# Q projection moved from a stage of its own into the attention stage's scratch tiles, interleaved with the first K/V pair

## The chip, the cores and the metric

One Trainium2 chip, all 8 cores, one launch. Each core runs the same program on its own data; the time is device microseconds of the slowest core. In the text PE is TensorE (matmuls, PEld its weight loads), DVE VectorE, ACT ScalarE, POOL GpSimd and SP SyncE. All loads are issued by SP on one hardware DMA queue; all stores by POOL on another.

## The reference, cut to what matters

A transformer layer with post-norm, in float32: batch 4, 2048 positions, 2048 features, 16 heads of 128.

```python
def attn(x, W_qkv, W_o):
    q, k, v = split(x @ W_qkv, 3)           # 16 heads of 128
    a = q @ k.T / sqrt(128) + alibi + causal
    return (softmax(a) @ v) @ W_o
x = layernorm(x + attn(x, W_qkv, W_o))
x = layernorm(x + ffn(x))                   # dense 2048x2048 + 16 low-rank experts, top 2
```

Core c holds batch c//2 and half of its query positions (eight tiles of 128, alternating so that the causal work is even): 1024 "own" positions. Each core projects Q for its 1024 positions, and K and V for all 2048.

## The kernel before, in words

A recording layer writes one list of operations for each engine (`Prog`); the kernel's order in the source is the order on each engine, and each engine runs its list strictly in that order. `Buf` (lines 69 to 115) holds for a buffer the semaphore counts that its next writer must wait for: `load` waits on SP for all recorded uses, then issues `split` DMAs, all at line 107; `store` issues on POOL at line 117.

- **Q stage** (lines 215 to 265). The core's whole input `xT_own` (8 MiB) is loaded into `xq` in 4 DMAs of 2 MiB. For each of 16 heads (`oc`) the 1 MiB of Q weights goes into one of two `wqb` buffers, by 4 DMAs of 256 KB, and is used for two banks of 512 positions, 16 contraction steps each (line 247). DVE scales a bank into `qout` (line 258), POOL stores it to `q_hbm`. Each float32 matmul appears as two records in the trace, so 512 matmuls are 1024 records.
- **Barrier** (line 266, `phase_barrier(q_done)`): every engine waits for all matmuls, all DVE and ACT work and all stores to `q_hbm`. The tiles of the next stage take the same memory.
- **K/V stage and attention** (from line 268). The generator `kv_gen(g)` (line 296) computes K and V for a pair of heads. Its first step only issues loads: `wk` 2 MiB, `wv` 2 MiB and two tiles of the input, `xb` 0 and 1, 2 MiB each. Then follow 32 steps: for each of 8 position tiles `tb`, two K steps (line 338) and two V steps (line 362), each 16 matmuls of 256 columns into bank 6 or 7, followed by a DVE copy. `xb` has two buffers: after the last step of tile `tb`, SP waits until PE has done it, then loads tile `tb+2` over it. `kv_gen(0)` runs alone (lines 517 to 519). Then `attention(gh, gen)` (line 424) runs eight times, with the steps of the next pair's generator woven between its own matmuls. It first loads `qh`, one head of Q from `q_hbm` (512 KB, after `q_done`), and lets the generator issue its loads; then per key tile it multiplies K with `qh` (line 455), adds the table `posb`, takes the exponential and multiplies with V (403) and with ones (412).
- The output projection, the layer norms, the router, the experts and the dense layer follow; the change does not touch them.

```python
def load(self, dst, src, split=1):
    ...
    self.begin_write()          # SP waits for every recorded use
    for i in range(split):
        mk = self.p.op("sync", ... e.dma_start(...), self.sem, 16)
```

Of the kernel before, what the change touches and what calls it, by code (L numbers as in the profile page):

```python
# [7 lines left out]
F32 = mybir.dt.float32  # L8
F16 = mybir.dt.float16
AF = mybir.ActivationFunctionType  # L10
ALU = mybir.AluOpType
# [3 lines left out]
H = 16  # L15
# [3 lines left out]
OWN = 1024  # L19
# [9 lines left out]
INV_SQRT_DH = 1.0 / float(np.sqrt(np.float64(DH)))  # L29
EPS = 1e-5  # L30
NEG_BIG = -1e30
FCN = 16
D3 = 3 * D
# [92 lines left out]
def build_program():  # L126
    nc = bass.Bass("TRN2", target_bir_lowering=False)

    xT = nc.dram_tensor("xT", [D, S], F32, kind="ExternalInput")
    xT_own = nc.dram_tensor("xT_own", [D, OWN], F32, kind="ExternalInput")  # L130
    x_own = nc.dram_tensor("x_own", [OWN, D], F32, kind="ExternalInput")
    wqkv = nc.dram_tensor("wqkv", [D, D3], F32, kind="ExternalInput")
# [14 lines left out]
    q_hbm = nc.dram_tensor("q_hbm", [D, OWN], F32)  # L147
# [5 lines left out]
    p = Prog()  # L153
    MM, DV, AC = "s_mm", "s_dv", "s_ac"

    def dap(t, offset, dims):
        return bass.AP(t, offset, dims)

    with ExitStack() as g:
# [55 lines left out]
        with ExitStack() as ph:  # L215
            def pb(name, shape, dt=F32):
                return ph.enter_context(nc.sbuf_tensor(name, shape, dt))

            xq = pb("xq", [128, FCN * 1024])
            xqb = B("sync")  # L220
            wqb = [pb(f"wqb{i}", [128, FCN * 128]) for i in range(2)]
            wqbuf = [B("sync"), B("sync")]
            qout = [pb(f"qout{i}", [128, 512]) for i in range(2)]
            qoutbuf = [B("vector"), B("vector")]

            xqmk = xqb.load(
                [dap(xq, fc0 * 1024, [[FCN * 1024, 128], [1024, 4], [1, 1024]])
                 for fc0 in range(0, FCN, 4)],
                [dap(xT_own, fc0 * 128 * OWN, [[OWN, 128], [128 * OWN, 4], [1, 1024]])
                 for fc0 in range(0, FCN, 4)], split=4)  # L230

            for oc in range(H):
                wb, wbuf = wqb[oc % 2], wqbuf[oc % 2]
                wmk = wbuf.load(
                    [dap(wb, fc0 * 128, [[FCN * 128, 128], [128, 4], [1, 128]])
                     for fc0 in range(0, FCN, 4)],
                    [dap(wqkv, fc0 * 128 * D3 + oc * 128,
                         [[D3, 128], [128 * D3, 4], [1, 128]])
                     for fc0 in range(0, FCN, 4)], split=4)
                for tb in range(2):  # L240
                    bi = (oc * 2 + tb) % 8
                    bb = bankbuf[bi]
                    bb.begin_write()
                    p.wait("tensor", wmk)
                    p.wait("tensor", xqmk)
                    for fc in range(FCN):
                        mmk = p.op("tensor", (lambda bi_, fc_, oc_, tb_: (lambda e: e.matmul(  # L247
                            banks[bi_][:, 0:512],
                            wqb[oc_ % 2][:, fc_ * 128:(fc_ + 1) * 128],
                            xq[:, fc_ * 1024 + tb_ * 512: fc_ * 1024 + tb_ * 512 + 512],  # L250
                            start=(fc_ == 0), stop=(fc_ == FCN - 1))))(bi, fc, oc, tb),
                            MM if fc == FCN - 1 else None)
                    wbuf.use(mmk)
                    bb.ready = mmk
                    qo, qob = qout[tb % 2], qoutbuf[tb % 2]
                    qob.begin_write()
                    p.wait("vector", mmk)
                    emk = p.op("vector", (lambda qo_, bi_: (lambda e: e.tensor_scalar(
                        qo_[:, :], banks[bi_][:, 0:512], INV_SQRT_DH, None,
                        ALU.mult)))(qo, bi), DV)  # L260
                    bb.use(emk)
                    qob.store(dap(q_hbm, oc * 128 * OWN + tb * 512,
                                  [[OWN, 128], [1, 512]]),
                              qo[:, :], deps=[emk])
            q_done = [qoutbuf[0].st_total(), qoutbuf[1].st_total()]
        phase_barrier(q_done)

        with ExitStack() as ph:
            def pb(name, shape, dt=F32):
# [8 lines left out]
            K2 = [pb(f"K2_{i}", [128, 2 * 2048]) for i in range(2)]  # L278
            V2 = [pb(f"V2_{i}", [128, 16 * 256]) for i in range(2)]
            k2buf = [B("vector"), B("vector")]  # L280
            v2buf = [B("vector"), B("vector")]
            qh = [pb(f"qh{i}", [128, 1024]) for i in range(2)]
            qhbuf = [B("sync"), B("sync")]
            posb = [pb(f"posb{i}", [128, 1024]) for i in range(2)]
            posbuf = [B("sync"), B("sync")]
            st_sb = [pb(f"st_sb{i}", [128, 1024]) for i in range(2)]
            stbuf = [B("vector"), B("vector")]
# [226 lines left out]
                                   deps=[last_y])  # L514

            gen0 = kv_gen(0)
            for _ in gen0:
                pass
            for gh in range(8):
                nxt = kv_gen(gh + 1) if gh < 7 else None  # L520
                attention(gh, nxt)
                if nxt is not None:
                    for _ in nxt:
                        pass
            y_done = [yfmsgbuf.st_total()]
        phase_barrier(y_done)
        with ExitStack() as cde:
# [58 lines left out]
            with ExitStack() as ph:  # L586
# [26 lines left out]
                for oc in range(FCN):  # L613
                    wbuf = wocb[oc % 2]
                    wmk = wbuf.load(
                        [dap(wocol[oc % 2], fc0 * 128,
                             [[FCN * 128, 128], [128, 4], [1, 128]])
                         for fc0 in range(0, FCN, 4)],
                        [dap(wo, fc0 * 128 * D + oc * 128,
                             [[D, 128], [128 * D, 4], [1, 128]])  # L620
                         for fc0 in range(0, FCN, 4)], split=4)
                    for tb in range(2):
                        bi = (oc * 2 + tb) % 2
                        bb = bankbuf[bi]
# [3 lines left out]
                        for fc in range(FCN):  # L628
                            mmk = p.op("tensor", (lambda bi_, fc_, oc_, tb_: (lambda e: e.matmul(  # L629
                                banks[bi_][:, 0:512],  # L630
                                wocol[oc_ % 2][:, fc_ * 128:(fc_ + 1) * 128],
                                yfm_all[:, fc_ * 1024 + tb_ * 512: fc_ * 1024 + tb_ * 512 + 512],
                                start=(fc_ == 0), stop=(fc_ == FCN - 1))))(bi, fc, oc, tb),
                                MM if fc == FCN - 1 else None)
# [20 lines left out]
                            start=(oc_ == 0), stop=(oc_ == FCN - 1))))(oc, tb),  # L655
# [11 lines left out]
                            start=(oc_ == 0), stop=(oc_ == FCN - 1))))(sq, oc, tb),  # L667
# [6 lines left out]
                for tt in range(NSLOT):  # L674
                    bi = tt % 2
                    bb = bankbuf[bi]
# [23 lines left out]
            with ExitStack() as ph:  # L700
# [35 lines left out]
                for tb in range(2):  # L736
                    bi = 6 + tb % 2
                    bb = bankbuf[bi]
# [13 lines left out]
                    if h_evacs:  # L752
# [14 lines left out]
                for tt in range(NSLOT):  # L767
                    bi = tt % 2
                    bb = bankbuf[bi]
# [42 lines left out]
                for tt in range(NSLOT):  # L812
                    bi = 2 + tt % 2
                    bb = bankbuf[bi]
# [3 lines left out]
                    for fc in range(FCN):  # L818
# [4 lines left out]
                            start=(fc_ == 0), stop=(fc_ == FCN - 1))))(bi, fc, tt),  # L823
# [9 lines left out]
                    wmk = None  # L833
# [6 lines left out]
                    for c in range(2):  # L840
# [19 lines left out]
            with ExitStack() as ph:  # L860
# [21 lines left out]
                for oc in range(FCN):  # L882
                    wbuf = wtcb[oc % 2]
# [212 lines left out]
```

How the kernel before makes its waits and increments, by code:

```python
            def run(e):  # L996
                for item in lst:
                    if item[0] == "wait":
                        e.wait_ge(sems[item[1]], item[2])
                    else:
                        _, fn, sem, by = item
                        ins = fn(e)
                        if sem is not None:
                            ins.then_inc(sems[sem], by)
```

## Time and profile before

| what | us |
|---|---|
| runs, median (lowest to highest of 3) | 5239.11 (4938.11 to 5711.35) |
| the profiled execution | 4931.57 |
| its span on the slowest core, core 0 | 4930.0 |
| spans of the 8 cores | 4892.6 to 4930.0 |
| PE busy, DVE busy, ACT busy on core 0 | 4225.8, 717.3, 411.6 |

The span runs from the first to the last instruction of one core; 1.6 us lie around it. Busy time is time in which an engine executes something; for PE it counts matmuls only. The granted clock of TensorE has two levels here, shown as 1.00 (2.4 GHz) and 0.50 (1.2 GHz); in a window it is a mean.

### The profile page before, as it was taken

How to read it: one execution, taken by the hardware profiler on the slowest of the kernel's cores; microseconds unless marked ns; L12 is line 12 of the kernel's file. 1: busy time of each engine (PE TensorE's matmuls, PEld its weight loads, DVE VectorE, ACT ScalarE, POOL GpSimd, SP SyncE). 2: the span in 40 equal slices, each digit the busy share in tenths (PEclk: the TensorE clock that was granted, in tenths of full speed). 3: DMA queues.
4: the chain of work that ended last, by engine and by line, in shares of the span. 5: the costliest groups of instructions: out<-in, count | busy, mean ns of one | idle time of the engine just before them, and what ended most of it. 6: DMA issues, size and time to landing. Idle time of an engine off the chain costs nothing.

```text
span 4930.0 us, 37169 instructions; the slowest of 8 cores (4892.6 to 4930.0 us)
## 1 busy us (share of the span) xinstructions
PE 4225.8 (86%) x14312; PEld 2728.1 (55%) x14312; DVE 717.3 (15%) x1152; ACT 411.6 (8%) x723; POOL 29.2 (1%) x56
## 2 busy tenths in 40 slices
PE   6998899879979989979989989977999556888882
PEld 3443787767767767767667767643344233333330
DVE  0000001111111111111111111130000332101115
ACT  0000001111111111111111111130000000000000
POOL 0000000000000000000000000000000000000000
PEclk9999999999999989999999999998999877889996
DMA  3211333232232232232232142123111001000001
GB/s 114 62 54 59 105 109 100 85 104 78 88 99 78 93 119 74 76 116 74 78 129 92 46 138 86 60 84 115 49 51 41 15 22 37 23 26 26 26 17 68
DMA packets 332846, 359.57 MB, mean 73 GB/s; under 512 B 16896, under 2 KB 293504, under 8 KB 332416
## 3 DMA queue, kind: packets, MB, share of 16 engines
q1 hardware_dynamic: 325696, 332.02, 21.5%
q0 software_dynamic: 6976, 25.17, 1.3%
q8 instruction: 116, 1.90, 0.2%
q14 instruction: 58, 0.48, 0.0%
HBM read 331.97 MB, written 25.17 MB: 72 GB/s over the span
## 4 chain that ended last, share of the span: by engine, by line
PE 84%; DVE 6%; SPq 4%; DMA 3%; issue 2%; ACT 0%; DVEq 0%; ACTq 0%; POOL 0%; POOLq 0%
PE bank L338 18%; PE bank L362 18%; PE bank L900 9%; PE bank L629 9%; PE bank L247 9%; PE bank L455 5%; PE bank L403 5%; PE bank L412 5%; SPq L107 4%; DMA xb<-xT 1%; PE bank L819 1%; DMA qh<-q_hbm 1%; PE bank L915 1%; PE bank L944 1%; PE bank L957 1%
## 5 line engine op out<-in xcount | busy, mean ns | idle before, releaser
L338 PE MATMUL bank<-xb,wk 128*128 128x256 f32 x4096 | 918.8, 384 | 156.4 <-DMA xb<-xT 156.4
L338 PEld LDWEIGHTS bank<-xb,wk 128*128 128x128 f32 x4096 | 790.8, 193 | 296.8 <-issue 187.2
L362 PE MATMUL bank<-wv,xb 128*128 128x256 f32 x4096 | 901.5, 379 | 0.0
L362 PEld LDWEIGHTS bank<-wv,xb 128*128 128x128 f32 x4096 | 775.0, 190 | 117.1 <-issue 3.3
L629 PE MATMUL bank<-yfm_all,wocol 128*128 128x512 f32 x1024 | 446.6, 594 | 41.1 <-DMA wocol<-wo 41.1
L900 PE MATMUL bank<-x1fm,wtcol 128*128 128x512 f32 x1024 | 470.1, 619 | 12.0 <-DMA wtcol<-wT 12.0
L247 PE MATMUL bank<-xq,wqb 128*128 128x512 f32 x1024 | 441.1, 594 | 38.5 <-DMA wqb<-wqkv 38.5
L455 PE MATMUL bank<-qh,K 128*128 128x512 f32 (+3 forms) x768 | 308.6, 512 | 81.3 <-DMA qh<-q_hbm 68.5
L900 PEld LDWEIGHTS bank<-x1fm,wtcol 128*128 128x128 f32 x1024 | 204.7, 200 | 277.7 <-issue 277.7
L629 PEld LDWEIGHTS bank<-yfm_all,wocol 128*128 128x128 f32 x1024 | 195.2, 191 | 286.8 <-issue 286.8
L247 PEld LDWEIGHTS bank<-xq,wqb 128*128 128x128 f32 x1024 | 195.1, 191 | 283.7 <-issue 283.7
L403 PE MATMUL bank<-pt_sb,V 128*128 128x512 f32 (+3 forms) x768 | 314.8, 492 | 32.9 <-ACT pt_sb L486 32.6
L486 ACT ACTIVATE pt_sb<-st_sb 128x1024 f32<-128x1024 f32 (+7 forms) x256 | 174.8, 683 | 1883.5 <-DVE st_sb L478 1883.5
L412 PE MATMUL bank<-pt_sb,ones_sb 128*128 128x512 f32 (+3 forms) x768 | 310.6, 486 | 0.0
L455 PEld LDWEIGHTS bank<-qh,K 128*128 128x128 f32 x768 | 149.3, 197 | 239.4 <-issue 228.6
L348 DVE COPY K<-bank 128x256 f32<-128x256 f32 x128 | 54.3, 424 | 1215.1 <-PE bank L338 1205.0
L478 DVE TENSOR_TENSOR st_sb<-st_sb,posb 128x1024 f32<-128x1024 f32 (+7 forms) x256 | 194.2, 759 | 149.0 <-ACT st_sb L465 101.6
L465 ACT COPY st_sb<-bank 128x512 f32<-128x512 f32 (+3 forms) x384 | 183.8, 479 | 333.2 <-PE bank L455 250.1
L372 DVE COPY V<-bank 128x256 f32<-128x256 f32 x128 | 54.3, 424 | 1037.9 <-PE bank L362 1018.9
L412 PEld LDWEIGHTS bank<-pt_sb,ones_sb 128*128 128x128 f32 x768 | 141.2, 190 | 112.4 <-issue 92.1
L403 PEld LDWEIGHTS bank<-pt_sb,V 128*128 128x128 f32 x768 | 138.9, 190 | 85.8 <-issue 63.7
L944 PE MATMUL bank<-x2fm,ones_sb 128*128 128x512 f32 x64 | 45.6, 802 | 85.3 <-DVE x2fm L935 85.3
(76 smaller groups left out, 932.6 us busy)
## 6 DMA issues: line engine op xcount, KB each, us to landing
xb<-xT SPq DMA_DIRECT2D x256, 512.0 KB, 6.5
wqb<-wqkv SPq DMA_DIRECT2D x64, 256.0 KB, 5.3
wk<-wqkv SPq DMA_DIRECT2D x32, 512.0 KB, 8.5
wv<-wqkv SPq DMA_DIRECT2D x32, 512.0 KB, 10.3
posb<-alibid SPq DMA_DIRECT2D x32, 512.0 KB, 8.7
wocol<-wo SPq DMA_DIRECT2D x64, 256.0 KB, 4.2
wtcol<-wT SPq DMA_DIRECT2D x64, 256.0 KB, 3.8
posb<-alibid SPq DMA_DIRECT2D x32, 448.0 KB, 3.3
```

Source lines behind the costliest of these rows:

```text
L107: mk = self.p.op("sync", (lambda d_, s_: (lambda e: e.dma_start(out=d_, in_=s_)))(dst[i] if split > 1 else dst, src[i] if split > 1 else s ...
L247: mmk = p.op("tensor", (lambda bi_, fc_, oc_, tb_: (lambda e: e.matmul(banks[bi_][:, 0:512], wqb[oc_ % 2][:, fc_ * 128:(fc_ + 1) * 128], x ...
L338: mmk = p.op("tensor", (lambda bi_, fc_, oc_, tb_, par_: (lambda e: e.matmul(banks[bi_][:, 0:256], wk_sb[par_][:, fc_ * 256 + oc_ * 128: f ...
L362: mmk = p.op("tensor", (lambda bi_, fc_, tt_, tb_, par_: (lambda e: e.matmul(banks[bi_][:, 0:256], xb[tb_ % 2][:, fc_ * 256 + tt_ * 128: f ...
L403: lambda e: e.matmul(banks[ybi_][:, co_: co_ + w_], V2[par_][:, kc_ * 256 + hd2_ * 128: kc_ * 256 + hd2_ * 128 + 128], pt_sb[kc_ % 2][:, r ...
L412: lambda e: e.matmul(banks[dbi_][:, co_: co_ + w_], ones_sb[:, :], pt_sb[kc_ % 2][:, ro_: ro_ + w_], start=st_, stop=sp_)))(dbi, kc, co, w ...
L455: lambda e: e.matmul(banks[bi_][:, 0:n_], K2[par_][:, hd2_ * 2048 + kc_ * 128: hd2_ * 2048 + kc_ * 128 + 128], qh[hd2_ % 2][:, s0_ * 128 + ...
L465: emk = p.op("scalar", (lambda bi_, kc_, ch_, n_: (lambda e: e.copy(st_sb[kc_ % 2][:, ch_ * 512: ch_ * 512 + n_], banks[bi_][:, 0:n_])))(b ...
L478: stmk = p.op("vector", (lambda kc_, w_: (lambda e: e.tensor_add(st_sb[kc_ % 2][:, 0:w_], st_sb[kc_ % 2][:, 0:w_], posb[kc_ % 2][:, 0:w_]) ...
L486: exmk = p.op("scalar", (lambda kc_, w_: (lambda e: e.activation(pt_sb[kc_ % 2][:, 0:w_], st_sb[kc_ % 2][:, 0:w_], AF.Exp)))(kc, w), AC)
L629: mmk = p.op("tensor", (lambda bi_, fc_, oc_, tb_: (lambda e: e.matmul(banks[bi_][:, 0:512], wocol[oc_ % 2][:, fc_ * 128:(fc_ + 1) * 128], ...
L900: mmk = p.op("tensor", (lambda bi_, fc_, oc_, tb_: (lambda e: e.matmul(banks[bi_][:, 0:512], wtcol[oc_ % 2][:, fc_ * 128:(fc_ + 1) * 128], ...
```

## The change

The Q stage, its tiles and the barrier behind it are removed. Q is now computed inside the attention stage, between the generator's first step and its end:

- The own positions are taken in two passes (`qp`) of 512, each as two halves (`qq`) of 256 that lie in `K2[1]` and `V2[1]`, the K and V buffers that pair 1 will use later. Each half is 2 MiB, in 4 DMAs of 512 KB.
- Q weights go through the two `qh` tiles, cut into four quarter buffers (`wq4`) of 256 KB, one for each four contraction steps (`fq`). Since there are two passes, all Q weights are loaded twice: 32 MiB, not 16.
- Per head, quarter and half there are 4 matmuls of 256 columns, into bank 0 or 1. After each quarter one step of `kv_gen(0)` is emitted. The generator has 32 such steps, so they are used up in the first 8 heads of the first pass; the other 24 head passes have nothing between their matmuls.
- After the four quarters DVE scales both banks into `st_sb`, and POOL stores them to `q_hbm`.
- The second pass reloads `K2[1]` and `V2[1]` when the first pass's last matmuls are done.

```diff
-            for oc in range(H):
-                wb, wbuf = wqb[oc % 2], wqbuf[oc % 2]
...
-                    for fc in range(FCN):
-                        mmk = p.op("tensor", (lambda bi_, fc_, oc_, tb_: (lambda e: e.matmul(
-                            banks[bi_][:, 0:512],
...
-        phase_barrier(q_done)
...
             gen0 = kv_gen(0)
+            next(gen0, None)
+            xq2 = [B("sync"), B("sync")]
+            xqt = [K2[1], V2[1]]
+            wq4 = [B("sync") for _ in range(4)]
...
+            for qp in range(2):
+                for qq in range(2):
+                    xq2[qq].load(
...
+                for oc in range(H):
+                    for fq in range(4):
+                        wb = wq4[fq]
+                        wt, woff = qh[fq // 2], (fq % 2) * 512
+                        wmk = wb.load(
...
+                        for qq in range(2):
+                            if fq == 0:
+                                bankbuf[qq].begin_write()
+                            p.wait("tensor", wmk)
+                            p.wait("tensor", xq2[qq].ready)
+                            for sub in range(4):
+                                fc = 4 * fq + sub
...
+                                        banks[qq_][:, 0:256],
...
+                            qqlast[qq] = mmk
...
+                        wb.use(mmk)
+                        next(gen0, None)
+                    for qq in range(2):
...
+                        p.wait("vector", qqlast[qq])
...
+                        bankbuf[qq].use(emk)
...
+                for qq in range(2):
+                    xq2[qq].use(qqlast[qq])
             for _ in gen0:
                 pass
```

**SP, from the start.** Before, in the order of issue: the input for Q, the Q weights of all heads, then K/V weights and input tiles (`xq` is the own input, `wqb` the Q weights, `xb` the input tiles of K/V).

```order
L107 DMA xq<-xT_own 128x4x1024 x4
L107 DMA wqb<-wqkv 128x4x128 x8
L107 DMA wqb<-wqkv 128x4x128 [waits s_mm]
L107 DMA wqb<-wqkv 128x4x128 x3
L107 DMA wqb<-wqkv 128x4x128 [waits s_mm]
L107 DMA wqb<-wqkv 128x4x128 x3
```

Now (`K_1` and `V_1` hold the own input, `qh` the Q weights; the wait on `s_mm` is one for matmuls):

```order
L107 DMA wk<-wqkv 128x4x256 x4
L107 DMA wv<-wqkv 128x4x256 x4
L107 DMA xb<-xT 128x4x256 x8
L107 DMA K_1<-xT_own 128x4x256 x4
L107 DMA V_1<-xT_own 128x4x256 x4
L107 DMA qh<-wqkv 128x4x128 x4
L107 DMA xb<-xT 128x4x256 [waits s_mm]
L107 DMA xb<-xT 128x4x256 x3
L107 DMA qh<-wqkv 128x4x128 x4
L107 DMA xb<-xT 128x4x256 [waits s_mm]
L107 DMA xb<-xT 128x4x256 x3
```

The first Q weights moved behind 12 MiB of other loads, and each head's Q weights stand behind an input tile's reload.

**PE, at the boundary of the first two heads of the first pass.** Before, PE goes from bank to bank of the Q stage with double-buffered weights:

```order
L247 MATMUL bank2<-xq,wqb1 128x512 x15
L247 MATMUL bank3<-xq,wqb1 128x512 x16
L247 MATMUL bank4<-xq,wqb0 128x512 [waits b6l]
L247 MATMUL bank4<-xq,wqb0 128x512 x15
L247 MATMUL bank5<-xq,wqb0 128x512 x16
```

Now (line 496 of the changed kernel is the Q matmul, 309 the V matmul and 285 the K matmul of the generator; `b11l` is the load of the first quarter buffer, `s_dv` DVE's work):

```order
L496 MATMUL bank0<-K2_1,qh1 128x256 [waits b14l]
L496 MATMUL bank0<-K2_1,qh1 128x256 x3
L496 MATMUL bank1<-V2_1,qh1 128x256 x4
L309 MATMUL bank7<-wv0,xb0 128x256 [waits s_dv]
L309 MATMUL bank7<-wv0,xb0 128x256 x15
L496 MATMUL bank0<-K2_1,qh0 128x256 [waits s_dv,b11l]
L496 MATMUL bank0<-K2_1,qh0 128x256 x3
L496 MATMUL bank1<-V2_1,qh0 128x256 [waits s_dv]
L496 MATMUL bank1<-V2_1,qh0 128x256 x3
L285 MATMUL bank6<-xb1,wk0 128x256 [waits b8l]
```

The Q matmuls of the next head stand right behind the tile's last V step, and ahead of the next K step.

**SP, at the end of the Q work.** Before, the loads of pair 1 follow the last input tile of `kv_gen(0)`:

```order
L107 DMA xb<-xT 128x4x256 [waits s_mm]
L107 DMA xb<-xT 128x4x256 x3
L107 DMA qh<-q_hbm 128x1024
L107 DMA wk<-wqkv 128x4x256 x4
L107 DMA wv<-wqkv 128x4x256 x4
```

Now (`b15s` and `b16s` are the stores of Q):

```order
L107 DMA K_1<-xT_own 128x4x256 [waits s_mm]
L107 DMA K_1<-xT_own 128x4x256 x3
L107 DMA V_1<-xT_own 128x4x256 [waits s_mm]
L107 DMA V_1<-xT_own 128x4x256 x3
L107 DMA qh<-wqkv 128x4x128 x4
L107 DMA qh<-wqkv 128x4x128 [waits s_mm] x60
L107 DMA qh<-q_hbm 128x1024 [waits b15s,b16s,s_mm]
L107 DMA wk<-wqkv 128x4x256 x4
L107 DMA wv<-wqkv 128x4x256 x4
L107 DMA xb<-xT 128x4x256 x8
```

The loads of pair 1, which were issued while `kv_gen(0)` still ran, now stand behind all Q weights and behind the last store of Q.

## Rows read from the trace of the kernel before

**Rows 1.** The page: busy time by engine, and the chain that ended last.

```profile
...
PE 4225.8 (86%) x14312; PEld 2728.1 (55%) x14312; DVE 717.3 (15%) x1152; ACT 411.6 (8%) x723; POOL 29.2 (1%) x56
...
PE 84%; DVE 6%; SPq 4%; DMA 3%; issue 2%; ACT 0%; DVEq 0%; ACTq 0%; POOL 0%; POOLq 0%
...
```

**Rows 2.** Waits of PE over the span (total us, times, longest us).

```profile
...
PE bank L338 <- DMA xb<-xT: 156.4, 7, 31.9
...
PE bank L247 <- DMA wqb<-wqkv: 38.5, 1, 38.5
...
```

**Rows 3.** Timeline from the start (start us, length us, operation).

```profile
...
3.19 7.38 SPq L107 DMA_DIRECT2D xq<-xT_own  x4
...
38.45 21.83 PE L247 MATMUL bank<-xq,wqb 128*128 128x512 f32 x47 [38.45 <-DMA wqb<-wqkv]
...
```

**Rows 4.** Timeline, end of the Q stage and start of K/V.

```profile
...
469.54 10.03 PE L247 MATMUL bank<-xq,wqb 128*128 128x512 f32 x23
...
479.75 0.69 DVE L258 TENSOR_SCALAR qout<-bank 128x512 f32<-128x512 f32 x1 [13.04 <-PE bank L247]
480.98 0.54 POOL L117 DMA_DIRECT2D q_hbm<-qout  x1 [13.20 <-DVE qout L258]
483.44 2.82 SPq L107 DMA_DIRECT2D wk<-wqkv  x4
...
511.48 16.17 PE L338 MATMUL bank<-xb,wk 128*128 128x256 f32 x64 [31.90 <-DMA xb<-xT]
...
527.48 13.98 PE L362 MATMUL bank<-wv,xb 128*128 128x256 f32 x64
...
541.29 13.98 PE L338 MATMUL bank<-xb,wk 128*128 128x256 f32 x64
541.63 0.42 DVE L372 COPY V<-bank 128x256 f32<-128x256 f32 x1 [6.48 <-PE bank L362]
...
```

**Rows 5.** Windows (us, busy us and records by engine, PEclk, DMA share, GB/s).

```profile
...
54.00:480.00 426.00, 425.58 (x992) 188.10 (x990) 21.67 (x32) 0.00 (x0) 16.92 (x31) 1.00 0.18 54
480.00:512.00 32.00, 0.53 (x1) 0.50 (x2) 0.45 (x1) 0.00 (x0) 0.54 (x1) 0.53 0.77 236
1991.00:1999.00 8.00, 0.01 (x1) 0.00 (x0) 6.93 (x4) 0.00 (x0) 0.22 (x1) 0.67 1.02 366
2001.00:2006.00 5.00, 5.00 (x16) 3.44 (x15) 0.00 (x0) 1.17 (x2) 0.00 (x0) 0.70 0.09 34
...
```

**Rows 6.** DMA of the stretch 500 to 520 us, in 40 slices.

```profile
...
GB/s 313 311 303 248 272 254 256 225 301 358 285 272 332 317 264 270 348 311 145 139 233 274 309 303 358 385 381 385 320 178 129 31 20 0 0 0 0 0 0 0
...
```

**Rows 7.** Timeline of SP, 540 to 552 us: one tile is reloaded.

```profile
...
541.54 2.60 SPq L107 DMA_DIRECT2D xb<-xT  x4
```

**Rows 8.** DMA of the stretch 540 to 552 us, in 40 slices.

```profile
...
GB/s 0 0 0 0 0 0 0 0 0 0 0 27 38 38 113 140 181 160 167 222 314 359 369 375 389 379 386 382 379 358 348 348 355 338 358 300 157 10 0 0
...
```

**Rows 9.** Timeline, 512 KB queued behind a tile, first of four.

```profile
...
919.77 3.19 SPq L107 DMA_DIRECT2D xb<-xT  x4
...
933.48 3.75 PE L455 MATMUL bank<-qh,K 128*128 128x512 f32 x4 [11.52 <-DMA qh<-q_hbm]
...
```

**Rows 10.** Timeline, the same, last of four.

```profile
...
1988.82 2.03 SPq L107 DMA_DIRECT2D xb<-xT  x4
...
1999.17 3.75 PE L455 MATMUL bank<-qh,K 128*128 128x512 f32 x4 [8.15 <-DMA qh<-q_hbm]
...
2010.25 1.88 PE L455 MATMUL bank<-qh,K 128*128 128x512 f32 x4
...
```

**Rows 11.** Timeline, start of attention for pair 1.

```profile
...
1065.82 0.43 SPq L107 DMA_DIRECT2D qh<-q_hbm  x1
...
1066.30 2.18 SPq L107 DMA_DIRECT2D wk<-wqkv  x4
...
1070.89 1.96 PE L455 MATMUL bank<-qh,K 128*128 128x512 f32 x4 [0.70 <-DMA qh<-q_hbm]
...
1095.49 16.00 PE L338 MATMUL bank<-xb,wk 128*128 128x256 f32 x64 [22.65 <-DMA xb<-xT]
...
```

**Rows 12.** The tile of the Q weights over the Q stage.

```profile
...
DMA to landing us min/median/max: 3.0/5.3/23.9
```

More of the change, by code:

```diff
@@ L213, in build_program @@
         zeromk = (DV, p.count[DV])
[L215 to L230, printed above, removed]
-            for oc in range(H):
-                wb, wbuf = wqb[oc % 2], wqbuf[oc % 2]
[L234 to L245, printed above, removed]
-                    for fc in range(FCN):
-                        mmk = p.op("tensor", (lambda bi_, fc_, oc_, tb_: (lambda e: e.matmul(
-                            banks[bi_][:, 0:512],
[L249 to L265, printed above, removed]
@@ L516, in build_program @@
             gen0 = kv_gen(0)
+            next(gen0, None)
+            xq2 = [B("sync"), B("sync")]
+            xqt = [K2[1], V2[1]]
+            wq4 = [B("sync") for _ in range(4)]
+            qo2 = [B("vector"), B("vector")]
+            qqlast = [None, None]
+            for qp in range(2):
+                for qq in range(2):
+                    xq2[qq].load(
+                        [dap(xqt[qq], fc0 * 256,
+                             [[4096, 128], [256, 4], [1, 256]])
+                         for fc0 in range(0, FCN, 4)],
+                        [dap(xT_own, fc0 * 128 * OWN + qp * 512 + qq * 256,
+                             [[OWN, 128], [128 * OWN, 4], [1, 256]])
+                         for fc0 in range(0, FCN, 4)], split=4)
+                for oc in range(H):
[3 more added lines that the diff above has]
+                        wmk = wb.load(
+                            dap(wt, woff, [[1024, 128], [128, 4], [1, 128]]),
+                            dap(wqkv, (4 * fq) * 128 * D3 + oc * 128,
+                                [[D3, 128], [128 * D3, 4], [1, 128]]))
+                        mmk = None
+                        for qq in range(2):
[5 more added lines that the diff above has]
+                                fc = 4 * fq + sub
+                                mmk = p.op("tensor", (lambda qq_, wt_, wo_, s_, fc_: (
+                                    lambda e: e.matmul(
+                                        banks[qq_][:, 0:256],
+                                        wt_[:, wo_ + s_ * 128: wo_ + s_ * 128 + 128],
+                                        xqt[qq_][:, fc_ * 256:(fc_ + 1) * 256],
+                                        start=(fc_ == 0), stop=(fc_ == FCN - 1))))(
+                                            qq, wt, woff, sub, fc),
+                                    MM if sub == 3 else None)
+                            qqlast[qq] = mmk
+                            if fq == 3:
+                                bankbuf[qq].ready = mmk
+                        wb.use(mmk)
+                        next(gen0, None)
+                    for qq in range(2):
+                        qob = qo2[qq]
+                        qob.begin_write()
+                        p.wait("vector", qqlast[qq])
+                        emk = p.op("vector", (lambda qq_: (lambda e: e.tensor_scalar(
+                            st_sb[qq_][:, 0:256], banks[qq_][:, 0:256],
+                            INV_SQRT_DH, None, ALU.mult)))(qq), DV)
+                        bankbuf[qq].use(emk)
+                        qob.store(dap(q_hbm, oc * 128 * OWN + qp * 512 + qq * 256,
+                                      [[OWN, 128], [1, 256]]),
+                                  st_sb[qq][:, 0:256], deps=[emk])
+                for qq in range(2):
+                    xq2[qq].use(qqlast[qq])
@@ L517, in build_program @@
             for _ in gen0:
                 pass
+            qlast = qqlast[1]
+            k2buf[1].use(qqlast[0])
+            v2buf[1].use(qqlast[1])
+            qhbuf[0].use(qlast)
+            qhbuf[1].use(qlast)
+            stbuf[0].use(qo2[0].st_total())
+            stbuf[1].use(qo2[1].st_total())
+            q_done = [qo2[0].st_total(), qo2[1].st_total()]
             for gh in range(8):
```

## The prediction

> **What bounds the kernel now.** I read the chain of waits first: it is PE for 84% of the span, and PE is busy for 4225.8 of 4930.0 us [rows 1]. So a change pays only where PE stands idle, and costs wherever it makes PE idle. The waits of PE say where: it waits 38.5 us at the very start for the first Q weights, and 156.4 us in 7 pieces for input tiles, the longest 31.9 us [rows 2]. The timeline puts that longest piece where the Q stage ends and K/V begins [rows 4]. In between PE has no gap: 425.58 of 426.00 us are busy, at the full granted clock, with the DMA engines used at 0.18 [rows 5]. The Q stage is thus hidden perfectly once it runs, and what can be won is the gap in front of it and the one behind it.
>
> **The removed barrier: -34.1 us.** The last Q matmuls end at 469.54 + 10.03 = 479.6 and the first K matmul starts at 511.48 [rows 4], 31.9 us. The clock is granted at 0.53 in that stretch [rows 5], and the first 64 records afterwards take 527.48 - 511.48 = 16.00 us, where the next 64 take 541.29 - 527.48 = 13.81: 2.2 us more. All of it goes, because K/V's loads now start with the kernel.
>
> **Narrower matmuls: +2.7.** Before, 992 records of 512 columns take 425.58 us, 0.429 each [rows 5], so 1024 take 439.3. Now there are 2048 of 256 columns, at 13.81 / 64 = 0.2158 [rows 4]: 442.0. Loading weights for half as many columns costs nothing, since the K and V steps already do just that. K and V themselves keep their 32 steps of 6.9 us.
>
> **The start: +14.5.** Before, 9 MiB are issued from 3.19 and PE starts at 38.45 [rows 3], 3.9 us per MiB. In the new order the first Q weights stand behind 12 MiB. The 8 MiB of 1 KB rows that begin at 483.44 [rows 4] have all come by 516.0, where the DMA falls silent [rows 6]: 4.1 us per MiB. For 12.25 MiB at 4.0 to 4.1 that is 49 to 50 us, so PE starts near 53 instead of 38.45. Bounds: 51 and 60 (the first 6 MiB at 483.44 needed 28.0 us until PE could start, 4.7 each).
>
> The Trainium skill, page "DMA: Bandwidth & Descriptors", section "Bandwidth", holds that two cores streaming from one HBM get about 358 GB/s each. By that figure, an estimate, 12.25 MiB would be in after 36 us and the start would cost nearly nothing: 5032 in all. The measured stretch moved 8 MiB in 32.6 us, some 257 GB/s, and the trace disagrees with the page here, so the sum doesn't use it.
>
> **Six stalls behind tile reloads: +76.8.** This is the largest term. During the first 8 heads the order is: last V step of tile tb, then, on SP, the wait for it, four DMAs of the next `xb` (2 MiB), and only then the first quarter of the next head's Q weights. On PE the very next instruction needs that quarter. A double-buffered tile that used to have 27.6 us to arrive now stands in front of something wanted at once. How long is that? When a tile is freed, at 541.29, SP issues the reload at 541.54 [rows 7], and the transfer ends in the slice at 551.1 [rows 8], 9.6 us later; 256 KB more at the 350 GB/s of those slices is 0.75, so the quarter is there 0.25 + 9.6 + 0.75 = 10.6 us after PE ran out. There is a direct model too: four times in the attention stage the 512 KB of `qh` are queued right behind a tile. From the tile's issue to PE's start it takes 933.48 - 919.77 = 13.7 us the first time [rows 9] and 1999.17 - 1988.82 = 10.35 the last [rows 10], the other two lie between. A load of `qh` that had nothing ahead of it was used after 5.1 us (1065.82 to 1070.89) [rows 11]. I take 10.6, bounds 9.5 and 13.7.
>
> Such an idle time also lowers the clock. In the 8 us ahead of 1999.17 the granted clock averages 0.67, between the two levels 1.2 and 2.4 GHz, and it is 0.70 in 2001 to 2006, with PE busy all through [rows 5]. The 4 + 32 records from 1999.17 to 2010.25 take 11.1 us [rows 10], against 4 x 0.429 + 32 x 0.2158 = 8.6 at full clock: 2.5. Together with 2.2 above and 16.00 - 13.98 = 2.0 after 22.65 us [rows 11], I take 2.2 for each; bounds 0 and 2.8. Tiles 2 to 7 are reloaded so, before heads 1 to 6: 6 x (10.6 + 2.2) = 76.8. The later quarters of a head come less than a microsecond apart and have 10.4 us of work each before them.
>
> **Two waits for DVE: +2.8.** DVE takes the V copy first and the scaling of bank 0 after it, and PE's next group needs bank 0. The copy starts 0.34 us after PE goes on (541.63 against 541.29) and takes 0.42 [rows 4]; scaling 256 columns takes about the same, with a tenth for each hand-over 1.4 us in all. At heads 1 to 6 it lies under the DMA stall; before heads 7 and 8 it is bare. Later, 4 matmuls (1.7 us) of the other half cover it.
>
> **The 24 head passes with Q alone: 0.** Each needs 1 MiB in 13.8 us. A quarter is reloaded when its 8 matmuls end and is wanted 3 x 3.45 = 10.4 us later; 256 KB land in 5.3 us, at best 3.0 [rows 12]. The 16 MiB read twice hide there. The 23.9 us of the longest landing are from the crowded start.
>
> **The turn between the passes: +19.2.** Both input halves, 4 MiB, are reloaded, SP issuing the first when the first half's matmuls end, 1.7 us before PE runs out. The next Q quarter stands behind both. Between 9.6 us for 2 MiB and 28.0 for 6 MiB, 4.25 MiB take 18.5 to 20; less 1.5 is 17 to 18.5. I take 17, bounds 13 and 20, and 2.2 for the clock. Nothing is left of K/V to cover it.
>
> **The start of attention: +32.9.** Before, the loads for pair 1 were issued under `kv_gen(0)`. Now SP first waits for the last store of Q: 3.9 us from PE's end, by the same chain at 479.6, DVE at 479.75, POOL at 480.98, SP at 483.44 [rows 4], less 0.3 for the shorter scaling. Then `qh`, and 0.5 later `wk`, `wv` and the first tile, 6 MiB. Pair 1's own attention shows just this: `wk` issued at 1066.30, first K matmul at 1095.49, 29.2 us [rows 11]. So K starts 3.6 + 0.5 + 29.2 = 33.3 us after PE ran out, of which 1.7 are the scores in between; a wait of 0.9 us that stood here goes; the clock adds 2.2. This nearly equals the barrier's 34.1: that gap is moved, not removed.
>
> **The sum.** 14.5 - 34.1 + 2.7 + 76.8 + 2.8 + 19.2 + 32.9 = 114.8. On the profiled execution's 4931.57 us that is 5046, a ratio of 1.023. That execution is near the lowest of the three runs, 4938.11; their median of 5239.11 contains two that lie 6 and 16% higher, and nothing in a 4930 us span explains those, so I forecast the undisturbed time.
>
> **The rivals.**
> *The small load passes the big one.* The DMA engines might finish a quarter while the tile ahead is still written. The Trainium skill, page "DMA: Bandwidth & Descriptors", section "Queues, rings and completion order", warns that completion is not first-in, first-out for an issuing engine. Price: the quarter is issued 0.25 + 2.6 us after PE's end and lands 3.0 to 5.3 later, so a stall is 5.9 to 8.2 instead of 10.6: 5018 to 5032, 5025 in the middle. Against it: `qh` needed 10.35 to 13.7 behind a tile [rows 9, 10] and 5.1 alone [rows 11].
> *Not slower.* The stalls don't arise, because the reload moves under the preceding V step: then only 14.5 - 34.1 + 2.7 + 2.8 + 19.2 + 32.9 = 38 us remain, 4970, 0.8% above and within what can be told. Even with the turn and the start of attention hidden as well it would be 4917, so faster by over 2% gets a chance only for a cover that I don't see. For it: the DMA engines are idle for 80% of this stage. Against: SP's reload waits for the tile's last matmul, and the program puts nothing between that and the quarter. Where the stall falls below 8 us, this decides the verdict.
> *The quarters are too small.* If a 256 KB load takes 13.4 us instead of 5.3, each of 24 head passes waits 3 us: 72 us more, 5118. The median landing [rows 12] speaks against it, the first case in rows 9, 13.7 us with a tile in front, shows it isn't absurd.
>
> **How the numbers follow.** About 2% is what a measurement of this kernel can tell from no change, 98.6 us here, close to my sum. Forecast 0.72, of which 0.10 fall under the 2%; the passing load 0.12, of which 0.10 under; not slower 0.08, of which 0.02 faster; quarters too small 0.08. Slower 0.72, same 0.26, faster 0.02. The bounds together: stalls 9.5 to 13.7 give -7 to +19, the clock -13 to +4, the start -2 to +7, the turn -4 to +3, attention -4 to +3. Not all at once: 5015 to 5080 for the forecast alone; to reach most of the other cases 4995 to 5100.
>
> **What would show each step right or wrong.** In the profile after, PE should first start near 53 us; six waits of Q matmuls for `qh`'s weights should be 10 to 11 us each, 55 us apart; one of about 17 us should stand between the passes, near 575; there should be no wait in the solo head passes; and the wait for `xb` at the start of attention should be over 20 us, as for the other pairs. Q's matmuls should sum to 442 us, plus what the low clock adds. A first start near 40, or waits behind tiles under 8 us, would make the prediction wrong, and so would gaps of a few microseconds in every solo head pass.

## The result and the profile after

The kernel became slower. Timed against the kernel before, the ratio is 1.018 (95% interval 1.010 to 1.026); timed again with the experiments it was 1.017 (1.009 to 1.025). Both intervals lie above 1, and both hold 1.02, so whether the loss is more than 2% stays open. The medians are 5211.3 us (8 runs, 5039.4 to 5784.2) against 5116.1 (10 runs, 4926.5 to 5711.4). Both medians, but not the ratio, include executions in which the cores of one die (0 to 3 or 4 to 7) were granted a lower TensorE clock for much of the time, as cores 0 to 3 were in the profiled execution of the kernel after. I therefore read cores 4 to 7 and compare each with the same core before: 5002.2, 5026.5, 5002.2 and 5037.6 us against 4914.7, 4927.4, 4901.3 and 4913.6. That is +87.5, +99.1, +100.9 and +124.0, +103 us in the mean.

The groups of PE on core 5 of the kernel after (busy us, mean ns of one | idle us before, and its releaser), which answer to [rows 2, 5]:

```profile
...
L285 PE MATMUL bank<-xb,wk 128*128 128x256 f32 x4096 | 921.8, 385 | 144.7 <-DMA xb<-xT 144.7
L309 PE MATMUL bank<-wv,xb 128*128 128x256 f32 x4096 | 902.8, 379 | 0.0
...
L496 PE MATMUL bank<-K,qh 128*128 128x256 f32 x1024 | 256.9, 396 | 142.7 <-DMA qh<-wqkv 139.9 <-DVE st_sb L512 2.8
L496 PE MATMUL bank<-V,qh 128*128 128x256 f32 x1024 | 245.6, 383 | 0.0
...
```

Q is the two rows of L496. Its matmuls are busy for 256.9 + 245.6 = 502.5 us, where the overlap of neighbours is counted to both rows (a group of 8 records lasts 1.89 us in the timeline, but the next starts after 1.73, and 256 groups at 1.73 make 442). The K and V rows, 921.8 and 902.8 us, had 921.7 and 901.4 on this core before. The new thing is the idle time: 139.9 us on loads of Q weights into `qh` and 144.7 on `xb`, where the same core of the kernel before had 37.9 and 162.0.

Each wait of Q for its weights is visible in the timeline of PE on the same core (start, length, operation, idle before it):

```profile
...
53.62 3.66 PE L496 MATMUL bank<-K,qh 128*128 128x256 f32 x8 [53.62 <-DMA qh<-wqkv]
...
111.31 3.75 PE L496 MATMUL bank<-K,qh 128*128 128x256 f32 x8 [14.32 <-DMA qh<-wqkv]
...
167.10 3.75 PE L496 MATMUL bank<-K,qh 128*128 128x256 f32 x8 [12.25 <-DMA qh<-wqkv]
...
222.53 3.75 PE L496 MATMUL bank<-K,qh 128*128 128x256 f32 x8 [10.78 <-DMA qh<-wqkv]
...
387.05 3.75 PE L496 MATMUL bank<-K,qh 128*128 128x256 f32 x8 [10.62 <-DMA qh<-wqkv]
...
432.34 1.97 PE L496 MATMUL bank<-K,qh 128*128 128x256 f32 x8 [1.39 <-DVE st_sb L512]
...
602.33 3.75 PE L496 MATMUL bank<-K,qh 128*128 128x256 f32 x8 [16.17 <-DMA qh<-wqkv]
...
```

And further on, at the start of attention:

```profile
...
823.80 1.89 PE L496 MATMUL bank<-V,qh 128*128 128x256 f32 x8
834.65 3.75 PE L402 MATMUL bank<-qh,K 128*128 128x512 f32 x4 [8.96 <-DMA qh<-q_hbm]
857.20 16.72 PE L285 MATMUL bank<-xb,wk 128*128 128x256 f32 x64 [18.79 <-DMA xb<-xT]
...
```

This is the order of the forecast. PE starts at 53.6 us. Six times, 54 to 58 us apart, the next head's first Q matmul waits for its quarter; two of the six, at 278.28 with 11.51 us and at 332.61 with 10.65, are left out. Then come two bare waits for DVE of 1.39 us (the first is shown), the wait between the passes, and at the start of attention one for `qh` and one for `xb`. The 3.75 us of the 8 records behind each DMA wait against 1.97 us behind the wait for DVE show the low clock after a gap: the 5 to 6 us behind the gaps that end at 111.31, 167.10 and 387.05 were granted 0.65, 0.54 and 0.61, and the 3.5 us from 432.34 on 1.00. On cores 4 to 7 the six waits sum to 66.8 to 72.0 us.

SP's row in one such gap shows the cause itself, the same core from 150 us on:

```profile
...
154.94 3.11 SPq L107 DMA_DIRECT2D xb<-xT  x4
158.09 6.62 SPq L107 DMA_DIRECT2D qh<-wqkv  x4
```

The tile is issued at 154.94, as soon as PE ran out (167.10 - 12.25 = 154.85), the quarters only from 158.09, and PE goes on 12.2 us after the tile's issue.

Finally the stages (us, busy us and records by engine, PEclk, DMA share, GB/s): the six gaps, the rest of the first pass, the second pass, attention.

```profile
...
54.00:432.00 378.00, 306.83 (x1344) 265.43 (x1343) 17.30 (x41) 0.00 (x0) 6.60 (x12) 0.91 0.20 58
432.00:586.00 154.00, 152.27 (x704) 133.59 (x704) 9.43 (x23) 0.00 (x0) 10.14 (x19) 1.00 0.24 70
602.00:823.00 221.00, 220.67 (x1013) 193.98 (x1014) 12.74 (x30) 0.00 (x0) 16.21 (x30) 0.99 0.31 91
834.00:3430.00 2596.00, 2343.91 (x9464) 1789.80 (x9464) 410.47 (x539) 359.46 (x639) 7.99 (x15) 0.95 0.28 92
...
```

Between 54 and 432 PE is busy for 307 of 378 us at a mean granted clock of 0.91; in the next two stretches it is busy all through but for the two waits for DVE, at 1.00 and 0.99, with the DMA engines at 0.24 to 0.31. The second reading of the weights costs PE no time there.

### The profile page after: what moved, and what is told of

The parts are those of the page before. It is cut to its first block, busy times and chain, and to the rows that moved or that the text cites. A ratio compares the mean times of both kernels' runs of the same rounds, so it can differ in the third digit from the quotient of the medians.

```text
span 5248.5 us, 39659 instructions; the slowest of 8 cores (5002.2 to 5248.5 us)
## 1 busy us (share of the span) xinstructions
PE 4448.5 (85%) x15336; PEld 3073.1 (59%) x15336; DVE 722.4 (14%) x1184; ACT 412.0 (8%) x723; POOL 46.5 (1%) x88
## 4 chain that ended last, share of the span: by engine, by line
PE 83%; DVE 6%; DMA 4%; SPq 4%; issue 2%; ACT 0%; DVEq 0%; ACTq 0%; POOL 0%; POOLq 0%
PE bank L285 18%; PE bank L309 18%; PE bank L496 11%; PE bank L913 9%; PE bank L642 8%; PE bank L402 5%; PE bank L350 5%; PE bank L359 4%; SPq L107 4%; DMA qh<-wqkv 1%; PE bank L832 1%; DMA xb<-xT 1%; DMA qh<-q_hbm 1%; PE bank L928 1%; PE bank L957 1%
## 5 line engine op out<-in xcount | busy, mean ns | idle before, releaser
L285 PE MATMUL bank<-xb,wk 128*128 128x256 f32 x4096 | 969.5, 399 | 137.7 <-DMA xb<-xT 137.7
L285 PEld LDWEIGHTS bank<-xb,wk 128*128 128x128 f32 x4096 | 825.0, 202 | 295.1 <-issue 171.2
L309 PE MATMUL bank<-wv,xb 128*128 128x256 f32 x4096 | 947.9, 392 | 0.0
L309 PEld LDWEIGHTS bank<-wv,xb 128*128 128x128 f32 x4096 | 806.2, 198 | 130.9 <-issue 5.2
L913 PE MATMUL bank<-x1fm,wtcol 128*128 128x512 f32 x1024 | 455.9, 604 | 12.4 <-DMA wtcol<-wT 12.4
L496 PE MATMUL bank<-K,qh 128*128 128x256 f32 x1024 | 303.0, 450 | 142.8 <-DMA qh<-wqkv 140.1
L402 PE MATMUL bank<-qh,K 128*128 128x512 f32 (+3 forms) x768 | 318.3, 526 | 88.6 <-DMA qh<-q_hbm 76.0
L496 PEld LDWEIGHTS bank<-K,qh 128*128 128x128 f32 x1024 | 233.5, 229 | 189.4 <-issue 146.8
L402 PEld LDWEIGHTS bank<-qh,K 128*128 128x128 f32 x768 | 152.6, 201 | 252.3 <-issue 241.8
L496 PE MATMUL bank<-V,qh 128*128 128x256 f32 x1024 | 295.6, 442 | 0.0
L496 PEld LDWEIGHTS bank<-V,qh 128*128 128x128 f32 x1024 | 231.9, 226 | 43.0
```

The source lines that it names most:

```text
L285: mmk = p.op("tensor", (lambda bi_, fc_, oc_, tb_, par_: (lambda e: e.matmul(banks[bi_][:, 0:256], wk_sb[par_][:, fc_ * 256 + oc_ * 128: f ...
L309: mmk = p.op("tensor", (lambda bi_, fc_, tt_, tb_, par_: (lambda e: e.matmul(banks[bi_][:, 0:256], xb[tb_ % 2][:, fc_ * 256 + tt_ * 128: f ...
L402: lambda e: e.matmul(banks[bi_][:, 0:n_], K2[par_][:, hd2_ * 2048 + kc_ * 128: hd2_ * 2048 + kc_ * 128 + 128], qh[hd2_ % 2][:, s0_ * 128 + ...
L496: lambda e: e.matmul(banks[qq_][:, 0:256], wt_[:, wo_ + s_ * 128: wo_ + s_ * 128 + 128], xqt[qq_][:, fc_ * 256:(fc_ + 1) * 256], start=(fc ...
```

## The experiments

Each kernel is the changed one with one edit, except the last. As stage marks I use the start of the last Q matmul and of the first score matmul (L402 in the changed kernel), since what happens behind them is not touched by most edits.

**The changed kernel again**, no edit, beside the first three variants.

> The changed kernel once more, beside the variants. Theory (queue position): spans of an undisturbed die near 5015 to 5040 us against some 4915 before; 8 waits of Q matmuls for the weights in the qh tiles: 53 us at the start, six of 10.6 to 14, one of 16. Rival (spread cost: the 256-column matmuls and 16 MiB more of weights slow everything a little): the waits would be the same, but Q's busy time would be well over 442 us plus what the low clock adds.

Spans of the eight cores were 4989 to 5077 us, ratio 1.017 (1.009 to 1.025). The six waits sum to 66.1 to 67.9 us on seven cores and to 72.2 on core 5, 68 in the mean; the first wait is 49.9 to 55.0, the one between the passes 15.4 to 16.6. On cores 4 to 7 the sums are within 5 us of those in the profile after. Nothing of the rival shows: the head passes with Q alone are at full rate.

**Quarters first.** The next head's quarters are issued ahead of the tile's reload.

```diff
-                        wmk = wb.load(
...
+                        wmk = wmks[fq] if wmks[fq] is not None else load_quarter(oc, fq)
...
                         wb.use(mmk)
+                        if fq == 3:
+                            wmks = [load_quarter(oc + 1, f_) if oc < H - 1 else None
+                                    for f_ in range(4)]
                         next(gen0, None)
```

> Only the order of loads on SP changes: the next head's four Q weight quarters are issued ahead of the tile reload. Theory: the six waits of 10.6 to 14 us and their 2 us of low clock go, six bare waits for DVE of 1.4 us come: -60 to -70 us against the changed kernel, spans near 4955. Rival (spread cost): the same bytes are moved, so within 15 us of the changed kernel.

The timeline of PE on core 0 of this kernel, only rows with a wait:

```profile
...
51.70 3.75 PE L500 MATMUL bank<-K,qh 128*128 128x256 f32 x8 [51.70 <-DMA qh<-wqkv]
...
97.59 1.96 PE L500 MATMUL bank<-K,qh 128*128 128x256 f32 x8 [1.40 <-DVE st_sb L519]
...
140.66 1.97 PE L500 MATMUL bank<-K,qh 128*128 128x256 f32 x8 [1.39 <-DVE st_sb L519]
...
355.99 1.97 PE L500 MATMUL bank<-K,qh 128*128 128x256 f32 x8 [1.39 <-DVE st_sb L519]
...
526.87 3.75 PE L500 MATMUL bank<-K,qh 128*128 128x256 f32 x8 [17.07 <-DMA qh<-wqkv]
...
```

All six DMA waits are gone, and 1.39 us for DVE stands in their place. Scores begin at 757.7 and 757.2 us on cores 0 and 3, against 832.1 and 831.7 in the repeat above; over cores 0 to 3 the last Q matmul comes 60 to 74 us earlier, 67 in the mean. On cores 4 and 5 it is 68 and 79 us, on 6 and 7 only 0.5 and 3.4, where the granted clock was 0.81 (last section). The ratio is 1.009 (1.003 to 1.014) instead of 1.017 (1.009 to 1.025). The same bytes move, so the spread cost is refuted: the largest term of the sum is the place in the queue. One thing got a little worse without any load added there: the wait between the passes is 16.1 to 19.2 us on the eight cores, against 15.4 to 16.6 in the repeat. Why is open.

**Half a tile ahead.** For pair 0, two of the tile's four DMAs are issued behind the first quarter.

```diff
+                    if g_ == 0 and 1 <= tb and tb + 1 < 8:
+                        xmks[tb + 1] = xhalf(tb + 1, 1)
...
-                            xmks[tb + 2] = xload(tb + 2)
+                            if g_ == 0:
+                                xhalf(tb + 2, 0)
+                            else:
+                                xmks[tb + 2] = xload(tb + 2)
```

> For pair 0 only two of the four DMAs of a tile's reload (1 MiB) stand ahead of the next head's first quarter, the other two are issued behind it. Theory (the wait is the time of what is queued ahead): the six waits fall from 10.6 to 14 by the transfer time of 1 MiB, 2.8 to 4 us, to 7 to 10: -17 to -24 us. Rival (the wait is latency from SP's late issue, not the bytes ahead): under 1 us each, -6 us at most.

The six waits sum to 47.0 to 59.0 us on the eight cores, 51 in the mean, against 68 in the repeat without the edit: 2.9 us less each for 1 MiB less ahead. The first of them on core 5:

```profile
...
94.78 0.92 SPq L281 DMA_DIRECT2D xb<-xT  x2
95.74 0.50 SPq L107 DMA_DIRECT2D qh<-wqkv  x1
96.29 1.05 SPq L281 DMA_DIRECT2D xb<-xT  x2
...
102.83 3.75 PE L514 MATMUL bank<-K,qh 128*128 128x256 f32 x8 [8.13 <-DMA qh<-wqkv]
...
```

PE ran out at 94.70; the quarter is issued at 95.74 and used at 102.83, 7.1 us later. There is no ratio for this kernel, but the waits suffice against the rival, which allowed less than 1 us each. They don't show that all of the 2.9 us are the MiB's transfer, for the edit has a second effect: SP issues two DMAs instead of four ahead of the quarter, and gets to it 1.05 us after PE ran out instead of 2.3 (means over the eight cores, this run and the repeat). At most 1.25 of the 2.9 us can be that, so a MiB ahead costs 1.6 to 2.9 us, and of the 11 us of a stall 3 to 6 are the tile's 2 MiB. The rest is the issue, by SP, of what stands ahead and of the quarter itself, and its landing. An order that issues the quarter in time removes all parts, as quarters first did.

**The turn covered.** The last four K/V steps are held back from head 7 and placed between the passes.

```diff
+                if qp == 1:
+                    for _ in gen0:
+                        pass
                 for oc in range(H):
...
                         wb.use(mmk)
-                        next(gen0, None)
+                        if oc < 7:
+                            next(gen0, None)
```

> The generator's last four steps (27.6 us of matmuls) are held back from head 7 of the first pass and put between the passes, over the reload of the own input. Theory: the wait of 16 us between the passes and its 2 us of low clock go, and one wait of 1.4 us for DVE: -19 us against the changed kernel. Rival: the reload takes longer than 27.6 us when K/V steps run beside it, and a part stays.

No wait stands between the passes on any of the eight cores. The last Q matmul starts at 797.5 to 805.1 us, against 815.2 to 827.0 in the repeat: -19 us in the mean, as expected, and the reload fits under 27.6 us of matmuls. Its spans, 4992 to 5057 us, don't show this gain: behind attention cores 0 to 3 took 1646 to 1650 us, against 1611 to 1621 in the repeat, with stretches at a granted clock of 0.81. There is no ratio for this kernel.

**Pair 1's loads spread over the second pass.**

```diff
+                    if qp == 1:
+                        if oc == 0:
...
+                            parts1, marks1 = kv_parts(1)
+                            todo1 = [f_ for k_ in ("wk", "x0", "wv", "x1") for f_ in parts1[k_]]
+                        todo1[oc]()
```

> Only the 16 loads of pair 1 (wk, wv, two input tiles) are issued one in each head of the second pass instead of all after it. Theory: the first K step of attention no longer waits over 20 us for xb; what stays is the wait for qh, about 9 us from the last Q matmul: -22 to -26 us against the changed kernel. Each added 512 KB in front of a quarter costs 1.5 us of its 5 us slack, so no new waits. Rival: the DMA engines are the limit in the second pass, quarters come late, up to 16 x 1.5 = 24 us lost, no gain.

Half right. The wait for `xb` at the start of attention is gone, and the first scores still wait 6.6 to 7.1 us for `qh` on cores 0 to 3, whose granted clock is as in the repeat. But from the last Q matmul to the last score of attention these cores win only 4 to 19 us against the repeat, 12 in the mean, and before that they lose 2 to 5 us. The loss has a visible place, on core 0:

```profile
...
590.15 1.64 SPq L253 DMA_DIRECT2D wk<-wqkv  x1
591.83 7.10 SPq L107 DMA_DIRECT2D qh<-wqkv  x4
...
602.10 3.75 PE L540 MATMUL bank<-K,qh 128*128 128x256 f32 x8 [19.33 <-DMA qh<-wqkv]
...
```

My first 512 KB for pair 1 stood ahead of the first quarter of the second pass, the mistake that the experiment was about: on cores 0 to 3 the wait between the passes is 17.4 to 19.3 us, where the repeat had 15.4 to 16.4. That the load is the whole cause isn't shown, since with quarters first this wait was up to 19.2 us without it. The ratio, 1.016 (0.989 to 1.044), says nothing.

**Q's loads first.**

```diff
-            gen0 = kv_gen(0)
-            next(gen0, None)
+            parts0, marks0 = kv_parts(0)
+            gen0 = kv_gen(0, marks0)
...
+                        if qp == 0 and oc == 0 and fq == 3:
+                            for k_ in ("wk", "x0"):
+                                for f_ in parts0[k_]:
+                                    f_()
```

> Only the start: the own input (4 MiB) and head 0's quarters are issued first, then wk and the first tile, then head 1's quarters with wv and the second tile; head 0 runs without K/V steps. Theory: PE starts near 22 us instead of 53.6 and waits about 3 us before head 1 (9.25 MiB at 4.1 us each): -25 to -29 us against the changed kernel. Rival: the wait only moves to head 1, as the K/V loads are as late as ever: less than 10 us gained.

PE starts at 21.2 and 24.5 us on cores 5 and 4 and waits 5.0 and 2.4 us before head 1. The last Q matmul starts at 793.8 and 802.4, against 825.3 and 817.9 in the profile after: -31.5 and -15.5 us, 23.5 in the mean, just under the expectation; on these two cores the rival, a gain of less than 10 us, falls. The ratio, 1.018 (0.999 to 1.037), doesn't show it. On cores 6 and 7 the mark is no earlier than in the kernel after (821.9 and 827.6), and there the granted clock was 0.81 or less from 55 to 210 us; cores 0 to 3 were granted 0.74 to 0.79 in the mean from 50 to 250 us.

**All of it together**, but for the half tile, with two more edits: DVE scales Q ahead of the V copy, and two K steps of pair 1 come ahead of the first scores.

```diff
                     if gen is not None and hd2 == 0:
-                        next(gen, None)
+                        for _ in range(2 if loaded else 1):
+                            next(gen, None)
```

> All edits together: Q loads first at the start, quarters ahead of tile reloads, DVE scales Q before it copies the V step (so no wait of 1.4 us), four K/V steps between the passes, pair 1's loads spread over the second pass, and two K steps of pair 1 ahead of the first scores. Theory: against the changed kernel -31 +3 (start), -77 (reloads), -3 (DVE), -19 (turn), -33 (attention): -160, spans near 4875 to 4885, faster than the kernel before by 30 to 40 us (0.7%). Rival (spread cost): stays above the kernel before.

The first and last start of the scores, on core 6, for the kernel before, the kernel after, and this one (columns: duration ns min/median/max, first and last start us, forms):

```profile
...
L455 PE MATMUL bank<-qh,K x768: 272/539/1194, 731.2 to 3306.0; 128*128 128x512 f32 x144, 128*128 128x384 f32 x16, 128*128 128x256 f32 x16, 128*128 128x128 f32 x16
...
```

```profile
...
L402 PE MATMUL bank<-qh,K x768: 272/539/1192, 825.0 to 3397.9; 128*128 128x512 f32 x144, 128*128 128x384 f32 x16, 128*128 128x256 f32 x16, 128*128 128x128 f32 x16
...
```

```profile
...
L440 PE MATMUL bank<-qh,K x768: 272/540/1194, 707.6 to 3245.5; 128*128 128x512 f32 x144, 128*128 128x384 f32 x16, 128*128 128x256 f32 x16, 128*128 128x128 f32 x16
...
```

On this core the last score starts 60.5 us earlier than before the change and 152.4 earlier than after it (152.8 against the repeat); on core 7 it is 43.4 and 157.1 us, of the 160 expected. The span of core 6 is 4847.3 us, against 4901.3 before. On the other six cores the last score is only 0 to 39 us earlier than before the change. The kernel as a whole is at 0.996 (0.989 to 1.003) of the kernel before: no difference that is measured, but the interval lies below that of the changed kernel, 1.009 to 1.025, so the edits took the loss back. One reason why cores 0 to 5 gained less is in the windows of this execution, core 6 and then core 4:

```profile
...
50.00:250.00 200.00, 200.00 (x928) 176.56 (x927) 12.31 (x29) 0.00 (x0) 5.41 (x10) 1.00 0.29 86
250.00:690.00 440.00, 440.00 (x2040) 388.45 (x2039) 26.75 (x63) 0.00 (x0) 27.02 (x50) 1.00 0.39 113
...
```

```profile
...
50.00:250.00 200.00, 200.00 (x795) 170.76 (x794) 10.19 (x24) 0.00 (x0) 4.32 (x8) 0.85 0.28 80
250.00:690.00 440.00, 440.00 (x2040) 387.34 (x2039) 27.18 (x64) 0.00 (x0) 25.94 (x48) 1.00 0.41 109
...
```

In both, PE is busy every microsecond from 50 to 250 us, but core 4 completes 795 records in it where core 6 completes 928, at a granted clock of 0.85 against 1.00: some 29 us are lost there, and 25 on cores 0 to 3 with their 810 or 811 records. Whether that is chance or what this early stage brings about, these runs don't settle. Against a simple rule that a stage without gaps is slowed: in the profile before, PE was busy without a gap from 100 to 400 us on all eight cores at 1.00, and in the profile after, cores 2 and 3 were granted about 0.75 in the mean in the same stretch in spite of the gaps.

## Why the prediction was right and wrong

The measured median, 5211 us, lies outside the range of 4995 to 5100, while the three lowest runs of the kernel after, 5039 to 5042 us, lie beside the forecast of 5046. The step that failed is the last sentence of "The sum", "so I forecast the undisturbed time": it put the executions that are longer at nothing, though two of the three runs of before were 6 and 16% longer, and 4 of the 8 runs after were over 5200. Either the value or the top of the range had to take that in. The second miss is the verdict. The chances leaned on "slower by over 2%" with 0.72; the ratio is 1.018, and "within 2%", given 0.26, is what it says, with an interval that holds both. A sum that ends 16 us above the bound doesn't carry 0.72 when one term alone is uncertain by that much.

The sum itself, +114.8, stands against +103 on cores 4 to 7. Until PE runs out of work ahead of attention its terms make 81.9, and these cores come there 85.2 to 89.7 us later than before, 88 in the mean; the attention stage adds 18 instead of 32.9, and what follows takes 3 off. So the profile comes 12 us under the forecast because one term was 15 too large and the stretch behind took 3 off, while the other terms together were 6 too small.

Term by term, forecast against measured on cores 4 to 7:

- The start, +14.5: first matmul at 50.9 to 53.7 instead of 36.6 to 37.9, +14.3 to +15.8. Right. The page of the Trainium skill that would have made this nothing ("DMA: Bandwidth & Descriptors", section "Bandwidth") isn't borne out by these rows.
- The barrier, -34.1: the gap of 32 us between the Q stage and K/V is gone on every core. Right; no run without the barrier alone was made, so its price is tested only in the sum.
- Narrower matmuls, +2.7: in the solo passes a group of 8 records follows the last every 1.73 us, 0.216 each, as forecast. Right.
- Six stalls, +76.8: 66.8 to 72.0 us of idle time where 63.6 were forecast, and 11.1 to 14.2 in all for the clock (the 16 Q records behind a gap take 1.5 to 3.1 us longer than 3.45), so 79 to 84. The edit "quarters first" took 67 of it back, which with the 6 x 1.4 us for DVE that it uncovers makes 75. Mechanism and size right; on cores 5 and 7 the first of the six is the long one, 14.3 and 14.2 us.
- Two waits for DVE, +2.8: 1.39 each. Right.
- The turn, +19.2: idle 15.4 to 16.2 and about 2 for the clock. Right, and 19 us came back when it was covered.
- The start of attention, +32.9: this is the term that was mis-sized. On core 5 the parts are as forecast: first K matmul 857.2 - 825.7 = 31.5 us after PE ran out, where 33.3 were forecast. Yet from the last matmul ahead of attention to its last score the stage grew by only 4 to 24 us, 18 in the mean; in the repeat it is 22 in the mean over the eight cores. The difference is in the later pairs: the six other waits for `xb` took 128.3, 129.6, 132.0 and 127.2 us on cores 4 to 7 before, and 115.5, 125.9, 109.3 and 119.3 after, 12 less in the mean. I priced this stall against an attention stage that stays as it was, and the later pairs gave part of it back. Why they do was not tested.
- Behind attention, forecast as nothing: -15.4, -14.6, +9.0 and +10.3 us on cores 4 to 7. There, counted in windows of 5 us from 3950 to 4900, the kernel before has 90 and 75 us at a granted clock of 0.81 on cores 4 and 5 and at most 10 on 6 and 7, and the kernel after has 105 and 75 on cores 6 and 7 and at most 5 on 4 and 5. At 0.19 of its length, an estimate, such a stretch costs 14 to 20 us, the size of the differences and with their signs.

Of the rivals, the small load that passes the big one is out (waits of 10.3 to 14.3, not 5.9 to 8.2); the half-tile run shows that the wait shrinks when less stands ahead. With it goes the reading of the Trainium skill's section "Queues, rings and completion order" ("DMA: Bandwidth & Descriptors") as a way past the queue. "Not slower" is out, as its condition, no stalls, is, and so are quarters that are too small: no wait in 24 solo passes but the one between the passes.

## What to carry to other kernels

Before a stage is woven into another, write down for each queue what stands directly ahead of every load that an in-order engine will want next; a small load behind a double-buffered tile turns a hidden transfer into a stall (here 10.3 to 14.3 us behind 2 MiB), and it comes back each round. A barrier that is removed is worth only the loads that can really start earlier: here K waited 31.5 us on core 5 at the start of the next stage, whose loads now stood behind the last store, and 18 to 22 us of the gain were lost again. And where runs of a kernel spread by 15%, forecast the ratio and the median time apart, and let the range of each say how many of the long executions it allows for.

## What was not expected of the hardware

The granted clock has a third value. In the variant with quarters first, two cores of one chip execute the same instructions in the same stage, core 0 and then core 6:

```profile
...
100.00:400.00 300.00, 290.28 (x1339) 253.47 (x1339) 17.84 (x42) 0.00 (x0) 7.10 (x14) 1.00 0.23 70
...
```

```profile
...
100.00:400.00 300.00, 291.64 (x1106) 245.17 (x1105) 14.86 (x35) 0.00 (x0) 6.63 (x12) 0.81 0.22 68
500.00:550.00 50.00, 50.00 (x234) 44.01 (x233) 3.40 (x8) 0.00 (x0) 4.33 (x8) 1.00 0.34 100
...
```

Core 6 is granted 0.81 and completes 1106 records in 292 busy microseconds, core 0 at 1.00 completes 1339 in 290; from 500 us on core 6 is at 1.00 as well. Its first scores come at 823.7 us instead of 757.7. Counted in windows of 10 us up to 4850 us, this value held for 10 to 160 us on the cores of the kernel before, for 400 us on core 6 here, and for 3400 to 4100 us on cores 4 to 7 of the kernel with pair 1's loads spread, whose spans are 5702 to 5808 us against 4984 to 5032 on its other cores. The Trainium skill, page "TensorE: Matmul & The Clock Gate", section "Seeing it yourself", describes a third state at 13/16 of the clock (0.81) that is set for a whole die. The level agrees with these rows; that it is the whole die's does not, since cores 4 and 5, of the same die as core 6, had none of it in this stage (core 4 completes 1340 records in the same window at 1.00; their last Q matmul starts at 751.2 and 748.0 us, core 6's at 814.7), and in the run with all edits cores 4 and 5 had it and 6 and 7 had not. It can move a single execution by more than any edit of this study, so stage marks on cores at the full clock told the variants apart where whole spans did not.
